# One maximum instruction for two heads, and a ring of two double banks, in the attention of a two-layer recurrent model

## What is computed

```
scores = einsum("bqhd,bkhd->bhqk", q, k) / sqrt(8)
attn   = softmax(scores, axis=-1)          # the maximum over k is subtracted first
o      = einsum("bhqk,bkhd->bqhd", attn, v)
```

## Time and profile before

| | before |
|---|---|
| median of 3 runs | 1397.99 us (1397.72 to 1400.63) |
| profiled execution | 1396.91 us, span 1395.1 us |
| PE busy | 925.4 us, 66% |
| DVE busy | 924.6 us, 66% |
| ACT busy | 601.5 us, 43% |
| POOL busy | 426.4 us, 31% |
| maxima on DVE (L1011) | 512 of 686 ns, 331.5 us |
| matmuls for maxima (L1104) | 1024 of 284 ns |
| granted TensorE clock | mean 0.842 of full |

### The profile page before, as it was taken

The page is one execution under the profiler, slowest core; times in us unless marked ns, Lnnn a source line. Parts: engine busy times, 40 slices in busy tenths (PEclk is TensorE's granted clock), DMA queues, the critical chain, the costliest instruction groups (busy, mean ns, idle before and its releaser), DMA issues. The chain is left out here.

```text
span 1395.1 us, 26838 instructions
## 1 busy us (share of the span) xinstructions
PE 925.4 (66%) x6948; PEld 603.3 (43%) x6949; DVE 924.6 (66%) x1959; ACT 601.5 (43%) x1187; POOL 426.4 (31%) x707
## 2 busy tenths in 40 slices
PE   1566348999998400588888602553999999766664
PEld 1333214555555400477777501331555555334443
DVE  8699536888885500255555375775788888579994
ACT  1476515666665000244444301662666666412221
POOL 5355301111110377355565411000111111034441
PEclk9987658999999555699999955875999999978886
DMA  6123395222220011111111030346232222000000
GB/s 238 61 100 126 99 413 173 59 57 48 58 58 2 12 53 53 36 43 43 43 43 41 22 100 20 106 165 136 49 59 56 49 58 58 2 1 15 15 15 16
DMA packets 109116, 97.62 MB, mean 70 GB/s; under 512 B 8194, under 2 KB 100997, under 8 KB 108822
## 3 DMA queue, kind: packets, MB, share of 16 engines
q1 hardware_dynamic: 99472, 69.33, 19.2%
q10 hardware_dynamic: 5254, 19.27, 3.5%
q0 software_dynamic: 4352, 8.57, 1.9%
HBM read 42.55 MB, written 54.32 MB: 69 GB/s over the span
## 5 line engine op out<-in xcount | busy, mean ns | idle before, releaser
L1011 DVE TENSOR_REDUCE neg_max<-bank 128x2 f32<-128x512 f32 x512 | 331.5, 686 | 112.7 <-PE bank L1104 112.0
L1074 ACT ACTIVATE pr<-score 128x512 f32<-128x512 f32 x512 | 278.1, 596 | 160.7 <-PE score L1144 160.6
L1104 PE MATMUL bank<-ks,qs 96*128 96x256 bf16 x1024 | 168.0, 284 | 28.3 <-DMA qs<-q_scratch 28.3
L1144 PE MATMUL score<-qs,ks 128*128 128x256 bf16 x1024 | 160.5, 280 | 23.7 <-DMA qs<-max_rows 21.6
L1158 PE MATMUL p_o<-pr,vs 128*9 128x256 f32 x2048 | 160.5, 385 | 0.4 <-ACT pr L1074 0.4
L974 POOL TENSOR_TENSOR max_parts<-neg_max,one 128x16 bf16<-128x16 f32 x64 | 13.8, 216 | 427.4 <-DVE neg_max L1011 427.4
L1144 PEld LDWEIGHTS score<-qs,ks 128*128 128x128 bf16 x1024 | 79.4, 98 | 145.8 <-ACT pr L1074 84.7
L1104 PEld LDWEIGHTS bank<-ks,qs 96*128 96x128 bf16 x1024 | 99.7, 101 | 50.6 <-issue 29.8
L1453 DVE TENSOR_SCALAR hid<-p_hd,b1c 128x128 f32<-128x128 f32 x144 | 43.9, 346 | 104.1 <-PE p_hd L1529 104.1
L1438 DVE TENSOR_SCALAR hn<-blk 128x128 f32<-128x128 f32 x72 | 52.6, 731 | 89.0 <-DMA blk<-h_scratch 88.8
L1520 PE MATMUL p_t<-cst,hn 128*128 128x128 f32 x72 | 24.2, 335 | 117.1 <-DVE hn L1438 116.9
(11 more groups left out here) (270 smaller groups left out, 1806.9 us busy)
## 6 DMA issues: line engine op xcount, KB each, us to landing
h_scratch<-blank ACTq DMA_DIRECT2D x1, 17556.0 KB, 52.5
ks<-k_scratch SPq DMA_DIRECT2D x64, 192.0 KB, 3.4
qs<-q_scratch SPq DMA_DIRECT2D x64, 192.0 KB, 3.9
k_scratch<-parts SPq DMA_DIRECT2D x16, 384.0 KB, 2.6
q_scratch<-parts SPq DMA_DIRECT2D x16, 384.0 KB, 2.6
blk<-h_scratch SPq DMA_DIRECT2D x72, 66.5 KB
w<-w_dram SPq DMA_DIRECT2D x2, 2048.0 KB, 10.4
k_scratch<-parts SPq DMA_DIRECT2D x16, 256.0 KB, 2.2
```

The source lines that it names most:

```text
L1011: dve.tensor_reduce(neg_max[:, i // HALF, :, i % HALF:i % HALF + 1], bk[:].rearrange("p (q t) -> p q t", t=L), AX.X, ALU.max, negate=True) ...
L1074: act.activation(pr[s % N_PR][:, 2 * k:2 * k + 2, :], score[k][:], ACT.Exp, scale=SCALE).then_inc(exp_done, 1)
L1104: last = pe.matmul(bk[:, qt * L:(qt + 1) * L], qs[u][0:MAX_ROW, i, qt * P:(qt + 1) * P], ks[u][0:MAX_ROW, i, :], start=True, stop=True)
L1144: last = pe.matmul(score[k][:, j, :], ks[u][:, h, kt * P:(kt + 1) * P], qs[u][:, h, :], start=True, stop=True)
```

## The change

A ring tile now has two PSUM banks (1024 columns), and the ring has two such tiles. One `max` use is a pair of heads: four matmuls, then one DVE instruction that reduces 1024 columns to four values per partition. `plan` has one max use in a step, and the rows use that stood between the two maxima of step 2 stands behind it. All other uses take one tile too, of which they use only the first bank. A full sequence now has 8 + 2 + 4 = 14 uses. POOL's, SP's and ACT's instructions are the same; the counts that they wait for follow the new numbering.

```diff
-        N_BANK, N_PR = 4, 4
+        N_BANK, N_PR = 2, 4
+        PAIRS = H // 2
...
-        bank = [S.ps(ctx, f"bank{i}", [P, 512]) for i in range(N_BANK)]
+        bank = [S.ps(ctx, f"bank{i}", [P, 2, 512]) for i in range(N_BANK)]
...
-        CARRIED = H - 2 * LATE
+        CARRIED = PAIRS - LATE
...
-            head = (2 * (s - LATE)) % H
             rows, rest = AT.get(s, ([], []))
-            uses = [("max", head)] + rows + [("max", head + 1)] + rest
+            uses = [("max", (s - LATE) % PAIRS)] + rows + rest
...
-                        split(b + 1, 0, left(b, "middle", ("max", HALF - 1)))
+                        split(b + 1, 0, left(b, "middle", ("max", PAIRS // 2 - 1)))
...
-                    dve.tensor_reduce(neg_max[:, i // HALF, :, i % HALF:i % HALF + 1],
-                                      bk[:].rearrange("p (q t) -> p q t", t=L), AX.X, ALU.max, negate=True
+                    at = 2 * i % HALF
+                    dve.tensor_reduce(neg_max[:, 2 * i // HALF, :, at:at + 2].rearrange("p q h -> p h q"),
+                                      bk.rearrange("p h (q t) -> p h q t", t=L), AX.X, ALU.max, negate=True
                                       ).then_inc(bank_free, 1)
...
-                    for qt in range(2):
-                        last = pe.matmul(bk[:, qt * L:(qt + 1) * L], qs[u][0:MAX_ROW, i, qt * P:(qt + 1) * P],
-                                         ks[u][0:MAX_ROW, i, :], start=True, stop=True)
+                    for j in range(2):
+                        h = 2 * i + j
+                        for qt in range(2):
+                            last = pe.matmul(bk[:, j, qt * L:(qt + 1) * L], qs[u][0:MAX_ROW, h, qt * P:(qt + 1) * P],
+                                             ks[u][0:MAX_ROW, h, :], start=True, stop=True)
```

More of the change, by code:

```diff
@@ L986, in _ @@
             copy_v(1, 1)
-            split(0, 0, left(0, "first", ("max", HALF - 1)))
-            split(0, 1, left(0, "start", ("max", H - 1)))
-            split(1, 0, left(0, "start", ("max", HALF - 1)))
+            split(0, 0, left(0, "first", ("max", PAIRS // 2 - 1)))
+            split(0, 1, left(0, "start", ("max", PAIRS - 1)))
+            split(1, 0, left(0, "start", ("max", PAIRS // 2 - 1)))
             if NB > 2:
@@ L993, in _ @@
                         b = pair * 2 + u + 1
-                        split(b, 1, left(b, "middle", ("max", H - 1)))
+                        split(b, 1, left(b, "middle", ("max", PAIRS - 1)))
                         pool.wait_ge(pr_free, b * STEPS + N_PR)
                         copy_v(b + 1, u)
-                        split(b + 1, 0, left(b, "middle", ("max", HALF - 1)))
-            split(NB - 1, 1, left(NB - 1, "last", ("max", H - 1)))
+                        split(b + 1, 0, left(b, "middle", ("max", PAIRS // 2 - 1)))
+            split(NB - 1, 1, left(NB - 1, "last", ("max", PAIRS - 1)))
         @block.vector
@@ L1018, in consume @@
                         dve.wait_ge(rows_in[i], 16 * c)
-                    dve.tensor_copy(max_rows[i][:], bk[0:3 * HALF, 0:L // 2].bitcast(BF16)).then_inc(bank_free, 1)
+                    dve.tensor_copy(max_rows[i][:], bk[0:3 * HALF, 0, 0:L // 2].bitcast(BF16)).then_inc(bank_free, 1)
                 else:
@@ L1027, in norm @@
                     sn.turn((c * 2 + stage) * 1)
-                    heads = bk[:].rearrange("p (h r) -> p h r", r=32)
+                    heads = bk[:, 0, :].rearrange("p (h r) -> p h r", r=32)
                     sn.link(dve.reciprocal(o_rec[:, stage, :].unsqueeze(2), heads[:, :, DK:VW]))
@@ L1033, in norm @@
                 elif stage == 2:
-                    dve.tensor_copy(o_t[:], bk[:, 0:L]).then_inc(bank_free, 1)
+                    dve.tensor_copy(o_t[:], bk[:, 0, 0:L]).then_inc(bank_free, 1)
                 else:
-                    proj = bk[:, 0:2 * D].rearrange("p (n c) -> p n c", c=D)
+                    proj = bk[:, 0, 0:2 * D].rearrange("p (n c) -> p n c", c=D)
                     two = bass.ds(2 * c, 2)
@@ L1099, in produce @@
                 if kind == "max":
-                    if i % HALF == 0:
-                        pe.wait_ge(operands_in[u][i // HALF], (c - u) * 16 + 32)
-                    for qt in range(2):
-                        last = pe.matmul(bk[:, qt * L:(qt + 1) * L], qs[u][0:MAX_ROW, i, qt * P:(qt + 1) * P],
-                                         ks[u][0:MAX_ROW, i, :], start=True, stop=True)
+                    if 2 * i % HALF == 0:
+                        pe.wait_ge(operands_in[u][2 * i // HALF], (c - u) * 16 + 32)
+                    for j in range(2):
[3 more added lines that the diff above has]
+                                             ks[u][0:MAX_ROW, h, :], start=True, stop=True)
                 elif kind == "rows":
@@ L1109, in produce @@
                     pe.sem_inc(turn_started, 1)
-                    turned = bk[0:3 * HALF, 0:L // 2].bitcast(BF16)
+                    turned = bk[0:3 * HALF, 0, 0:L // 2].bitcast(BF16)
                     for qt in range(2):
@@ L1118, in produce @@
                     for hg in range(HG):
-                        last = pe.transpose(bk[:, hg * P:(hg + 1) * P], o_raw[:, hg, i * P:(i + 1) * P], S.ident)
+                        last = pe.transpose(bk[:, 0, hg * P:(hg + 1) * P], o_raw[:, hg, i * P:(i + 1) * P], S.ident)
                 elif i == 2:
@@ L1123, in produce @@
                     for qt in range(2):
-                        last = pe.transpose(bk[:, qt * P:(qt + 1) * P],
+                        last = pe.transpose(bk[:, 0, qt * P:(qt + 1) * P],
                                             o_n[:, qt].rearrange("p h d -> p (h d)"), S.ident)
@@ L1128, in produce @@
                     for qt in range(2):
-                        last = pe.matmul(bk[:, qt * D:(qt + 1) * D], o_t[:, qt * P:(qt + 1) * P],
+                        last = pe.matmul(bk[:, 0, qt * D:(qt + 1) * D], o_t[:, qt * P:(qt + 1) * P],
                                          S.m(("wo", "proj")[layer]), start=True, stop=True)
```

## The result

| | before | changed |
|---|---|---|
| median | 1397.86 us (4 runs) | 1444.07 us (4 runs, 1442.74 to 1445.06) |
| ratio | | 1.0328, 95% interval 1.0309 to 1.0347 |
| profiled execution | 1396.91 us, span 1395.1 | 1444.13 us, span 1442.3 |
| PE busy | 925.4 us | 934.6 us |
| DVE busy | 924.6 us | 909.8 us |

The changed kernel is 46.2 us slower. Forecast were 1440 us, that is 42.3 us more, and a range of 1428 to 1456. DVE has 15 us less to do, and the kernel gained nothing from it.

What follows compares the result with a forecast made beforehand. PE was taken to bound the kernel in attention. Terms of 1.19 + 0.16 + 0.15 = 1.50 us per middle sequence, x 28 = 42.0, + 0.3 = 42.3 us, led to 1440 us, range 1428 to 1456.

Steps and rivals of the forecast that it cites:

- Norm 1's wait: Step 2: norm 1 needs the tile of the maxima just before it; +1.19 us a middle sequence. Rival, no wait: 0.03.
- PE sets the pace: Attention: PE busy 165.97 of 170 us, DVE has spare time; DVE's saving of 17 us gains nothing.
- The double maximum: On DVE: takes 1.22 us, starting 0.64 us after its first matmul. Rival, 1.89 us and 1552 in all: chance 0.07.
- The next use of the tile: On PE: the next matmul needing the same tile can begin 1.95 us after the maxima's first matmul.
- Step 3: Step 3 to step 4: the maxima of step 4 need the tile of step 3's; 1.95 instead of 1.79, +0.16 us.
- rows 0: Step 5: PE waits for POOL's parts, which start behind step 4's last maximum, now ending later; +0.15 us.
- Steps 1 and 4: Same pattern as step 3, but step 1 lasts 1.97 us anyway; both at nothing, with only 0.02 of cover.
- The transfer of rows 1: Rows 1 to the scores of step 4: the later copy stays hidden, 0.6 us of cover from norm 1's wait.
- First and last sequences: Outside the middle sequences: the first has rows 0 but no norm, +0.15 twice; the last does not change.
- The spread: Range of the main case: 1.25 to 1.85 us a sequence, 35 to 52 us, 1433 to 1450.
- the clock: Rival: PE's rests lower the clock, one plain step a sequence at half speed, 43 us more, 1483; chance 0.05.
- The last rival: No change: counted in PSUM banks the ring held four and still holds four; time stays 1398; chance 0.03.

Runs made afterwards that it cites:

- rows_first: The changed kernel with step 2's uses in the order rows 1, maxima, norm 1: 1411.34 us.
- half_maximum: The changed kernel, whose maxima read only the first 128 of the 256 keys of each head: 1403.03 us.
- values_before_waits: The changed kernel with the values of the step before moved ahead of norm 1 in step 2 and of rows 0 in step 5: 1417.73 us.
- mixed_tiles: The changed kernel with double maxima kept, but every other use takes a single bank of the second double tile: 1434.67 us.
- single_two: The kernel before with the ring cut from four single banks to two, and no double instruction: 1498.59 us.
- before_values_first: The kernel before the change, with the values of the step before ahead of rows 0 in step 5 on PE: 1383.41 us.

## Why the prediction was right

The mechanism was the one forecast. Norm 1's wait alone makes 28 x 1.22 = 34 of the 46 us, and rows_first and half_maximum move the time by moving or shortening this wait. By the prediction's own steps:

- *PE sets the pace.* Right: a wait on PE appeared in full in the time, and 15 us less work on DVE gave nothing. values_before_waits shows it from the other side. PE's share fell to 91%; 89% was forecast.
- *The double maximum takes 1.22 us and starts 0.64 after the first matmul.* 1.226 and 0.64. The price of a column, taken from two reductions, and the row that reads two banks were the right neighbours; the reduction of 1890 ns was not.
- *The next use of the tile after 1.95 us.* 1.92 at norm 1 and at the maxima of step 4 (1137.35 to 1139.27). The 0.03 us from the weight load to its matmul, an estimate that named no row, was 0.00 at both places.
- *Norm 1, +1.19.* +1.22. Two small errors partly cancelled: norm 1 starts 0.03 earlier than forecast, and the values follow it after 0.59 us (1135.76 to 1136.35), not 0.53.
- *Step 3, +0.16; rows 0, +0.15.* +0.13 and +0.11.
- *Steps 1 and 4 at nothing, with 0.02 of cover.* This term was mis-sized: +0.08 and +0.05, 3.6 us in all. In step 1 it is norm 0, which was named as a place with 0.02 of cover: its tile comes free too late for the weight load, which PE made 0.1 us ahead before the change (see the last section). In step 4 no maximum of the next step waits. The matmuls of norm 3 take 0.59 us to the values instead of 0.54; they need DVE's copy of norm 2 and its tile. Why they lose 0.05 was not tested.
- *The transfer of rows 1 is hidden, with 0.6 us of cover from norm 1's wait.* Right; mixed_tiles took the cover away, and the transfer cost 0.69 us.
- *First and last sequences, +0.3.* Too small. The two profiled executions differ by 47.2 us, so 2.7 lie outside the middle sequences. The forecast gave the first sequence only the delay of rows 0. But that sequence has no norm 1 to cover the transfer of rows 1, and the scores of step 4 waited for it already. In layer 1, before and after the change:

```profile
984.39 0.61 PE L1144 MATMUL score<-qs,ks 128*128 128x256 bf16 x4 [0.49 <-DMA qs<-max_rows]
```

```profile
1008.49 0.61 PE L1147 MATMUL score<-qs,ks 128*128 128x256 bf16 x4 [1.17 <-DMA qs<-max_rows]
```

  That is +0.68 us in this layer, the same effect that mixed_tiles brought into every middle sequence.
- *The spread.* Its upper end of 1.85 us a sequence leaves out the 0.1 that the same sentence gives to the places with little cover. The measured 1.59 lies inside either way.

The sum was 4.9 us short of the profiled 47.2: 0.09 us in each of 28 middle sequences, 2.5 in all, and 2.4 outside them.

Of the rivals, the clock stayed at 1.00 through the waits in the middle sequences of both layers (230 to 460 us and 1060 to 1230), the double maximum was not slow, and norm 1 did wait. The last rival was to count PSUM banks, by which nothing is lost. It falls with the result, and once more with rows_first: the kernel uses all 8 banks with and without that line, and the two differ by about 32 us. How many releases can be outstanding, and in which order they are asked for, decided the time. The rule to use all 8 banks stands in the Trainium skill ("Perfetto Trace Analysis", section "Matmul Optimizations"); these runs show that it was not enough here. Another section of that page of the Trainium skill ("Optimizing Tensor Performance") asks that independent matmul groups rotate through different banks, so that the reading out of one overlaps the matmuls of the next. single_two agrees: rotating through two banks instead of four cost 102 us.

## What to carry to other kernels

Merging two instructions into one saves time of their engine, and here that engine was not the bound. Look first at which engine has no idle time before its groups. A merged instruction holds its buffers longer, and with the same memory the ring has fewer of them. So follow each ring use back by the ring's size to the use that holds its tile, and price the wait: the end of that holder, plus the release, less the time at which the use's own turn would come.

If an engine works in order and a wait can't be avoided, put work that is ready in front of it. Before removing a wait, look up which transfer it has been covering, and check whether some sequence never had that cover.

## What was not expected of the hardware

- A wait of which the profile lists nothing on PE can still cost. Norm 0 of step 1 in the changed kernel, from PE's weight loads:

```profile
1131.69 0.43 PEld L1107 LDWEIGHTS bank<-ks,qs 96*128 96x128 bf16 x4
1132.25 0.42 PEld L1122 LDWEIGHTS bank<-cst,o_raw 128*128 128x128 f32 x4
```

  The loads of the maxima end at 1132.12; the next one starts 0.13 later, together with its transpose (1132.26). In the kernel before it started at 1111.38 for a transpose at 1111.48, 0.10 ahead. The four f32 transposes then take 0.58 us to the values instead of 0.53, and start 0.47 us after the maxima instead of 0.44. It is the same in every middle sequence looked at, and 0.08 us a sequence went there. DVE ends the maximum that holds the tile at 1130.90 + 1.23 = 1132.13, just when the load would have started 0.1 us ahead. That the late release is the reason is read from these times; no run tested it.
- The wait that the profile lists on PE is shorter than the time lost. It counts from the end of the record before, and the next group can start before that end: the maxima's record lasts 0.60 us, and rows follow them after 0.54 when nothing holds them (1133.84 to 1134.38). In step 5 before the change the rows started 0.93 us after the maxima (1119.07 to 1120.00), so 0.39 us were lost where 0.33 is listed. The other 0.08 of the 0.47 us that before_values_first gained come from the new order. Maxima, rows, values, scores without a wait take 0.54 + 0.15 + 0.56 = 1.25 us (1120.00 to 1120.15 to 1120.71), and maxima, values, rows, scores took 1.17 (1123.12 to 1124.29). Likewise the 1.11 us listed at norm 1 cost 1.22.
